# Replicating state-space channels: a stride of eight, in two transfers of 2 KB rows

## The chip, the cores and the metric

The kernel runs on one core of one Trainium2 chip. The metric is the device time of one execution in microseconds, the median over several runs. TensorE, VectorE, ScalarE and GpSimd (PE, DVE, ACT and POOL in the profile) compute; SyncE (SP) only issues DMAs, which run on the core's 16 DMA engines.

## The reference

The input `x` is [8, 256, 128]. It is normalised, and goes through two branches whose results are combined as `x + s * silu(f)`. One, `f`, is a six-layer local-attention transformer. The other, `s`, is one Mamba block, and it is the one that the change touches (D = 256 channels, N = 16 states, DTR = 16):

```
proj = h @ in_W + in_b
x1, g = (proj[..., :D], proj[..., D:])
...
dbc = x1 @ dbc_W + dbc_b
delta, Bm, Cm = (dbc[..., :DTR], dbc[..., DTR:DTR + N], dbc[..., DTR + N:])
delta = jax.nn.softplus(delta @ dup_W + dup_b)
A_disc = jnp.exp(delta[..., None] * A)
B_x = delta[..., None] * Bm[:, :, None, :] * x1[..., None]
...
def step(hc, inp):
    a, b = inp
    hc = a * hc + b
    return (hc, hc)
...
y = jnp.einsum('tbdn,btn->btd', hs, Cm)
y = jax.nn.silu(g) * y
out = y @ out_W + out_b
```

## The kernel before

Every engine has its own program, and semaphores order them. `start_phase` loads and normalises, `main_phase` does nearly all the work, `gate_phase` combines the branches. `main_phase` is a software pipeline over `i` in `FIRST_TO_LAST`: step `s` is one batch element in one of six layers, 48 steps in all, and each engine's loop body is a list, written out by hand, of calls such as `scores(i, 2)` or `z_decay(i - 7, 10)`. The attention of a step is, on TensorE, `qk` (L559), `value` (L575), four transposes `turn` (L584), `scores` (L596 and L604, 8 and 32 small matmuls in one call), `turn_p` (L616), `values_out` (L633, 32 small matmuls) and `w_out` (L648). Those many small matmuls make most of TensorE's 30944 instructions.

The Mamba branch is spread between them: batch `b` begins at step 6b. `du` holds, for each of the 128 partitions (channels c * 128 + p), 1024 numbers: the step sizes `delta` for two blocks c and 256 tokens, and then their products `u = delta * x1`. The scan has a row for each channel and state, so 16 channels at a time are replicated eight times over the partitions: `replicate(s, n)` on SyncE (L488 to L502) sends 16 rows of `du`, 4 KB each, to the 128 partitions of `rep[:, slot]`, partition 8d + z from row d, one DMA of 512 KB. There are eight of them for a batch, 64 in all, in four slots. `ROWS16` gives the order of the groups, and `chunk(j)` names, for each of 16 chunks, the group and which half of the 16 states the eight copies stand for. A slot is used by `z_decay` (ACT, L1015, exp of delta times A) and by `z_bu` (POOL, L1380, u times B); the semaphore `rep_in[slot]` goes up by 16 when a DMA has landed. Then come `z_scan` (DVE, L1215), `z_hc` (POOL, L1391) and `z_sum` (TensorE, L744), which sums the eight copies of a channel into a row of `Y`; `z_gate`, `z_out` and `z_state` finish the batch.

SyncE's list also holds `spread` (L422, 14 copies V<-V for a step, 64 KB each, before `values_out` can run), `arrange_x` (L436, XV<-XT), the weights of the next layer (L135 to L150) and `replicate_bc` (L482, L486), which doubles the rows of B and C from 8 to 128 partitions by a chain of DMAs; the last of them (64 partitions, `n = 4`) is issued just behind `replicate(·, 2)`, and POOL's first `z_bu` of a batch waits for it (semaphore `bc_in`). SyncE issues in order, and all its DMAs go through one queue of the profile, q1. TensorE's own instructions are also brought in by DMA: the profile lists them as q8, those of the other engines as q14.

Of the kernel before, what the change touches and what calls it, by code (L numbers as in the profile page):

```python
# [19 lines left out]
P = 128  # L20
LN_EXP = "natural_log_exp_and_others"
NB, SEQ, DM = 8, 256, 128
# [7 lines left out]
DI, NST, KC, DTR = 256, 16, 4, 16  # L30
DBLK = DI // P
# [8 lines left out]
BSTEP = 6  # L40
NAB = 12
NREP = 4
NH = 5
ZSUM = 2
ROWS16 = (0, 2, 4, 6, 1, 3, 5, 7)
# [243 lines left out]
def main_phase(nc, t, k, R, T, C0, X, M, Y):  # L289

    with ExitStack() as ctx:
# [42 lines left out]
        du = m.sb("du", [P, 2, DBLK, SEQ])  # L334
        delta, u = du[:, 0], du[:, 1]
        rep = m.sb("rep", [P, NREP, 2, DBLK, SEQ])
# [19 lines left out]
        rep_in = [m.sem(f"rep_in{n}") for n in range(NREP)]  # L356
# [15 lines left out]
        def is_batch(s):  # L372
            return 0 <= s < STEPS and s % BSTEP == 0

        def chunk(j):

            n = 2 * (j // 4) + j % 2
            return n, ROWS16[n], (j // 2) % 2
# [10 lines left out]
        def m_free(eng, kind, n, s):  # L389

            before = M_BEFORE[kind, n, s]
            if before is not None:
                kind, n, s = before
                b = s // BSTEP
                sem, count = {"z_x": (conv_done, b + 1), "z_g": (g_copied, 2 * b + 2), "z_dbc": (dbc_copied, b + 1),
                              "z_dup": (dx_copied, 2 * b + 2), "z_out": (st_done, b + 1),
                              "z_decay": (scan_done, 16 * b + n + 1)}[kind]
                eng.wait_ge(sem, count)
# [6 lines left out]
        block = ctx.enter_context(nc.Block())  # L405

        @block.sync
        def _(sp):
# [79 lines left out]
            def replicate(s, n):  # L488

                if not is_batch(s):  # L490
                    return
                b = s // BSTEP
                sp.wait_ge(delta_done, b + 1)
                k = 8 * b + n - NREP
                if k >= 0:
                    chunks = 16 * (k // 8) + 4 * (k % 8 // 2) + 3 + k % 2
                    sp.wait_ge(dA_done, chunks)
                    sp.wait_ge(bu_done, chunks)
                r = 16 * ROWS16[n]
                sp.dma_start(rep[:, (8 * b + n) % NREP].rearrange("p z c t -> p (z c t)"),  # L500
                             du[r:r + 16].rearrange("d (o z) c t -> d o (z c t)", o=1).broadcast_to([16, 8, 2 * DBLK * SEQ]))\
                  .then_inc(rep_in[(8 * b + n) % NREP], 16)  # L502

            for i in FIRST_TO_LAST:
                replicate(i - 4, 2)
                next_qk(i, 1)
                replicate(i - 7, 5)
                replicate_bc(i - 3, 0)
                replicate(i - 6, 4)
                replicate_bc(i - 4, 4)  # L510
                replicate(i - 3, 0)
                next_v(i, 0)
                arrange_x(i + 2)
                replicate(i - 7, 6)
                replicate(i - 7, 7)
                replicate_bc(i - 3, 1)
                replicate_bc(i - 3, 2)
                spread(i, 0)
                next_qk(i, 2)
                replicate(i - 5, 3)  # L520
                replicate(i - 3, 1)
                spread(i, 1)
                next_qk(i, 3)
                next_v(i, 1)
                spread(i, 2)
                next_qk(i + 1, 0)
                replicate_bc(i - 3, 3)
                spread(i, 3)
                other_weights(i)
# [293 lines left out]
        def _(act):  # L823
# [157 lines left out]
            def z_copy_dx(s):  # L981
                if not is_batch(s):
                    return
                b = s // BSTEP
                act.wait_ge(zu_full, b + 1)
                if b > 0:
                    for n in range(NREP):
                        act.wait_ge(rep_in[n], 16 * ((8 * b - n + NREP - 1) // NREP))
                for c in range(DBLK):
                    act.activation(delta[:, c, :], M[:, c * SEQ:(c + 1) * SEQ], ACT.Identity, bias=dupb[:, c:c + 1])\  # L990
                       .then_inc(dx_copied, 1)
# [13 lines left out]
            def z_decay(s, j):  # L1005

                if not is_batch(s):
                    return
                n = 16 * (s // BSTEP) + j
                r, rows, half = chunk(j)  # L1010
                act.wait_ge(rep_in[(8 * (s // BSTEP) + r) % NREP], 16 * ((8 * (s // BSTEP) + r) // NREP + 1))
                m_free(act, "z_decay", j, s)
                for c in range(DBLK):
                    col = 16 * c + 2 * rows + half
                    ins = act.activation(M[:, c * SEQ:(c + 1) * SEQ], rep[:, (8 * (s // BSTEP) + r) % NREP, 0, c, :], ACT.Exp,  # L1015
                                         scale=Aneg[:, col:col + 1])
                ins.then_inc(dA_done, 1)
# [3 lines left out]
            for i in FIRST_TO_LAST:  # L1021
                copy_p(i - 1, 3)
                copy_v(i, 1)
                z_decay(i - 8, 13)
                z_tap(i + 1)
                z_decay(i - 4, 1)
                z_decay(i - 6, 6)
                copy_qk(i, 0)
                copy_v(i, 2)
# [12 lines left out]
                z_decay(i - 5, 3)  # L1042
                square(i + 1, 2)
                z_copy_dx(i - 1)
                z_decay(i - 7, 8)
                z_exp_x(i)
# [246 lines left out]
        def _(pool):  # L1293
            links = [0]

            def link(ins):

                links[0] += 1
                ins.then_inc(pool_link, 1)
                pool.wait_ge(pool_link, links[0])  # L1300
# [55 lines left out]
            def z_delta(s):  # L1356

                if not is_batch(s):
                    return
                b = s // BSTEP  # L1360
                pool.wait_ge(ln_done, 2 * b + 2)
                if b > 0:
                    for n in range(NREP):
                        pool.wait_ge(rep_in[n], 16 * ((8 * b - n + NREP - 1) // NREP))
                link(pool.tensor_tensor(delta, delta, se[:], ALU.add))
                pool.tensor_tensor(u, delta, x1s[:], ALU.mult).then_inc(delta_done, 1)

            def z_bu(s, j):

                if not is_batch(s):  # L1370
                    return
                b = s // BSTEP
                n = 16 * b + j
                r, _, half = chunk(j)
                pool.wait_ge(rep_in[(8 * b + r) % NREP], 16 * ((8 * b + r) // NREP + 1))
                if j == 0:
                    pool.wait_ge(bc_in, BC_IN * (b + 1))
                if n >= NH:
                    pool.wait_ge(zy_full, (n - NH) // ZSUM + 1)
                pool.tensor_tensor(hb[:, n % NH], rep[:, (8 * b + r) % NREP, 1],  # L1380
                                   BC[:, 0, half:half + 1, :].broadcast_to([P, DBLK, SEQ]), ALU.mult).then_inc(bu_done, 1)
# [22 lines left out]
            for i in FIRST_TO_LAST:  # L1404
                z_hc(i - 6, 4)
                normalise(i, 0)
                normalise(i, 1)
                z_bu(i - 7, 8)
                z_hc(i - 8, 12)
                rotate_sum(i, 6)  # L1410
                z_bu(i - 4, 2)
                normalise(i, 2)
                z_bu(i - 7, 9)
                normalise(i, 3)
                normalise(i, 4)
# [34 lines left out]
                z_hc(i - 8, 15)  # L1450
                z_bu(i - 4, 3)
                z_delta(i - 2)
                z_bu(i - 4, 4)
                z_hc(i - 7, 11)
# [130 lines left out]
def mamba_vectors(g):  # L1585

    def cols(a):
        return a.reshape(-1, P, *a.shape[1:]).swapaxes(0, 1).reshape(P, -1)
    return np.concatenate([cols(g[n]) for n in ("in_b", "conv_b", "dup_b", "out_b", "rms_w", "conv_w")], 1)


def decay_rows(a):

    return a.reshape(DBLK, 8, 16, 2, 8).transpose(2, 4, 0, 1, 3).reshape(P, DBLK * NST)


def layer_vectors(g):

    v = np.zeros((P, DEPTH, NVEC), np.float32)
    for k, name in enumerate(("ln_g", "ln_b", "b2")):  # L1600
        v[:, :, k] = g[name].T
    for c, (f0, n) in enumerate(FFC):
        for h in range(2):
            v[:n, :, 3 + 3 * h + c] = g["b1"][:, h * FFI + f0:h * FFI + f0 + n].T
    return v
# [24 lines left out]
```

## Time and profile before

| | |
|---|---|
| median of 3 runs | 1931.85 us (1925.41 to 1934.93) |
| profiled execution, own time | 1930.3 us |
| its span | 1928.5 us |
| PE busy | 1756.7 us (91%) |
| DVE busy | 1596.1 us (83%) |
| POOL busy | 1527.8 us (79%) |
| ACT busy | 1252.5 us (65%) |
| TensorE's mean granted clock | 0.971 of full speed |
| DMA queue q1, share of 16 engines' span | 31.1% |
| rep<-du, 64 DMAs of 512 KB, issue to landing | 7.3 us |
| V<-V, 672 DMAs of 64 KB, issue to landing | 2.1 us |

Busy is the time in which an engine executes something; the shares are means over the whole span. A granted clock of 1.0 is 2.4 GHz and of 0.5 is 1.2 GHz. "issue" as the end of a wait means that the engine waited for nothing that the profile can name.

### The profile page before, as it was taken

What the parts mean: (1) busy time and instruction counts of PE and PEld (TensorE: products, weight loads), DVE (VectorE), ACT (ScalarE), POOL (GpSimd) and SP (SyncE); (2) the same over time, 40 slices, a digit from 0 to 9 for tenths busy, and PEclk for the clock granted to TensorE, in tenths of its full rate; (3) what the DMA queues carried; (4) which work ended last, traced back from release to release, by engine and by line L of the source; (5) the groups of instructions that cost most, each with busy time, mean ns of one, the idle gap of its engine ahead of it and who ended that gap; (6) DMA issues with size and microseconds to landing.
All of it is one profiled execution on the core that took longest, in us unless ns stands there. A gap on an engine that the chain in (4) does not pass through costs nothing. (4 is left out here: it accounts for less than half of the span.)

```text
span 1928.5 us, 73996 instructions
## 1 busy us (share of the span) xinstructions
PE 1756.7 (91%) x30944; PEld 999.4 (52%) x30944; DVE 1596.1 (83%) x2736; ACT 1252.5 (65%) x2339; POOL 1527.8 (79%) x1348
## 2 busy tenths in 40 slices
PE   3798999999999999999999999999999999999862
PEld 1355555555555555555555555555555555555420
DVE  5777998888888897889988898889878798888536
ACT  3566676676676676776776676676766666766630
POOL 1765899878998789878998789888888689987640
PEclk9999999999999999999999999999999999999975
DMA  3114234153313334142332433342331534123321
GB/s 109 29 39 70 45 71 79 37 85 49 66 33 67 72 61 71 41 71 55 68 71 37 87 49 59 74 79 39 67 58 33 100 62 63 30 45 58 54 23 44
DMA packets 95607, 113.14 MB, mean 59 GB/s; under 512 B 42334, under 2 KB 61548, under 8 KB 95276
## 3 DMA queue, kind: packets, MB, share of 16 engines
q1 hardware_dynamic: 95276, 108.41, 31.1%
q8 instruction: 246, 4.03, 0.9%
q14 instruction: 85, 0.70, 0.1%
HBM read 19.22 MB, written 1.05 MB: 11 GB/s over the span
## 5 line engine op out<-in xcount | busy, mean ns | idle before, releaser
L1315 POOL TENSOR_TENSOR AB<-qc,qn 128x512 f32<-128x512 f32 x384 | 494.6, 1298 | 21.4 <-DVE qn L1109 21.4
L1326 POOL TENSOR_TENSOR AB<-AB,rinv 128x512 f32<-128x512 f32 x384 | 402.0, 1062 | 24.5 <-DVE rinv L1132 24.5
L559 PE MATMUL bank<-wqkv,XT 128*128 128x512 f32 x768 | 400.2, 614 | 12.2 <-DVE qn L1109 12.2
L1333 POOL TENSOR_TENSOR Pb<-Pb,p_rden 128x512 f32<-128x512 f32 x192 | 200.1, 1042 | 235.2 <-DVE p_rden L1153 234.1
L848 ACT ACTIVATE qkT<-bank 128x512 f32<-128x512 f32 x384 | 229.2, 597 | 209.3 <-PE bank L584 208.6
L1109 DVE TENSOR_TENSOR qc<-bank,rt 128x512 f32<-128x512 f32 x384 | 261.3, 680 | 123.4 <-ACT sq L839 108.9
L584 PEld LDWEIGHTS bank<-ident,AB 128*128 128x128 f32 x1536 | 181.7, 142 | 181.9 <-issue 119.3
L839 ACT ACTIVATE sq<-bank 128x512 f32<-128x512 f32 x384 | 228.1, 594 | 66.4 <-PE bank L559 57.3
L1109 DVE TENSOR_TENSOR qn<-bank,rt 128x512 f32<-128x512 f32 x384 | 261.4, 681 | 0.0
L584 PE MATMUL bank<-ident,AB 128*128 128x128 f32 x1536 | 241.5, 280 | 13.3 <-ACT qkT L848 6.2
L1116 DVE TENSOR_REDUCE ssq<-sq 128x8 f32<-128x512 f32 x384 | 251.2, 670 | 0.0
L633 PEld LDWEIGHTS bank<-PT,V 64*64 64x64 f32 x12288 | 198.3, 135 | 76.1 <-issue 73.4
L633 PE MATMUL bank<-PT,V 64*64 64x32 f32 x12288 | 219.9, 221 | 13.5 <-issue 8.9
L575 PE MATMUL bank<-wqkv,XV 128*128 128x512 f32 x384 | 196.2, 613 | 3.0 <-DVE qn L1109 3.0
L863 ACT ACTIVATE PT<-bank 128x512 f32<-128x512 f32 x192 | 114.3, 595 | 121.9 <-PE bank L616 118.8
L604 PE MATMUL bank<-qkT 64*32 64x64 f32 x12288 | 167.2, 223 | 23.9 <-issue 23.9
L1215 DVE TENSOR_TENSOR_SCAN hb<-bank,hb 128x256 f32<-128x256 f32 x256 | 161.3, 672 | 29.2 <-ACT bank L1015 29.0
L648 PE MATMUL bank<-OT,wo 128*128 128x512 f32 x384 | 182.2, 598 | 2.4 <-DVE XT L1190 2.4
L1380 POOL TENSOR_TENSOR hb<-rep,BC 128x512 f32<-128x512 f32 x128 | 165.2, 1297 | 17.1 <-PE bank L744 8.6
L1391 POOL TENSOR_TENSOR hb<-hb,BC 128x512 f32<-128x512 f32 x128 | 162.2, 1275 | 20.3 <-DVE hb L1215 20.0
L1139 DVE TENSOR_REDUCE mx<-bank 128x8 f32<-128x512 f32 x192 | 130.3, 679 | 45.6 <-PE bank L604 43.0
L604 PEld LDWEIGHTS bank<-qkT 64*32 64x32 f32 x12288 | 151.3, 105 | 24.6 <-issue 24.4
(137 smaller groups left out, 2657.3 us busy)
## 6 DMA issues: line engine op xcount, KB each, us to landing
V<-V SPq DMA_DIRECT2D x672, 64.0 KB, 2.1
rep<-du SPq DMA_DIRECT2D x64, 512.0 KB, 7.3
wqkv<-in_Wqkv SPq DMA_DIRECT2D x36, 256.0 KB, 3.7
XV<-XT SPq DMA_DIRECT2D x96, 64.0 KB, 2.8
wo<-in_Wo SPq DMA_DIRECT2D x6, 512.0 KB, 4.1
BC<-BC SPq DMA_DIRECT2D x8, 256.0 KB
w<-in_W SPq DMA_DIRECT2D x6, 341.0 KB, 3.2
BC<-BC SPq DMA_DIRECT2D x8, 128.0 KB
```

The costliest lines, as they stand in the source:

```text
L559: pe.matmul(R[u % 2][:], XT[:, s % NB, (u % 2) * P:(u % 2 + 1) * P], wqkv[:, (u // 2) * 512:(u // 2 + 1) * 512], start=True, stop=True).th ...
L575: pe.matmul(R[n % 2][:], XV[:, q % 2, s % 2, tl, :], wqkv[:, c:c + 512], start=True, stop=True)\
L584: mm = pe.transpose(T[:, c * P:(c + 1) * P], AB[:, (8 * s + u) % NAB, c * P:(c + 1) * P], ident[:])
L604: mm = pe.matmul(SB[w * WIN:(w + 1) * WIN, odd, col:col + 2 * WIN], qkT[p0:p0 + DH, g % 2, c, WIN + tok:2 * WIN + tok], qkT[p0:p0 + DH, g ...
L633: mm = pe.matmul(OB[DH * odd:DH * (odd + 1), tl, c * P + w * WIN:c * P + (w + 1) * WIN], V[r, w, h0:h0 + DH], PT[r, g % 2, 2 * odd + c, w ...
L839: act.activation(sq[:, u % 2, :], R[u % 2][:], ACT.Square).then_inc(sq_done, 1)
L848: act.activation(qkT[:, g % 2, :, WIN + tl * P:WIN + (tl + 1) * P], T.rearrange("p (c t) -> p c t", c=4), ACT.Copy).then_inc(qkT_done, 1)
L1109: ins = dve.tensor_tensor(out if z == 0 else out[:, :, :, ::-1, :], src, tab, ALU.mult)
L1116: dve.reduce_sum(ssq[:, 8 * u:8 * u + 8], sq[:, u % 2, :].rearrange("p (h d) -> p h d", d=DH), AX_X)\
L1315: pool.tensor_tensor(AB[:, n % NAB, :], qc[:, u % 2, :], qn[:, u % 2, :], ALU.add).then_inc(rs_done, 1)
L1326: pool.tensor_tensor(o, o, r, ALU.mult).then_inc(nm_done, 1)
L1333: pool.tensor_tensor(Pb[:, g % 2], Pb[:, g % 2], r, ALU.mult).then_inc(pn_done, 1)
```

## The change

`replicate` takes the channels r, r + 8, ..., r + 120 of `du` instead of 16r to 16r + 15, and issues two DMAs instead of one: first `delta` (2 KB for each of the 128 rows), then `u` (2 KB). Both raise the same semaphore, so its waits count 32 for a slot instead of 16. What stands in which partition of `rep` has changed, so the host lays out the decay table, the gate's columns of `in_W` with their bias, and the rows of `out_W` in the new order; their sizes and loads stay as they are.

```
                 r = ROWS16[n]
                 for z in range(2):
                     sp.dma_start(rep[:, (8 * b + n) % NREP, z].rearrange("p c t -> p (c t)"),
                                  du[r::8, z].rearrange("d (o c) t -> d o (c t)", o=1).broadcast_to([16, 8, DBLK * SEQ]))\
                       .then_inc(rep_in[(8 * b + n) % NREP], 16)
...
-                        act.wait_ge(rep_in[n], 16 * ((8 * b - n + NREP - 1) // NREP))
+                        act.wait_ge(rep_in[n], 32 * ((8 * b - n + NREP - 1) // NREP))
...
-                pool.wait_ge(rep_in[(8 * b + r) % NREP], 16 * ((8 * b + r) // NREP + 1))
+                pool.wait_ge(rep_in[(8 * b + r) % NREP], 32 * ((8 * b + r) // NREP + 1))
...
-    return a.reshape(DBLK, 8, 16, 2, 8).transpose(2, 4, 0, 1, 3).reshape(P, DBLK * NST)
+    return a.reshape(DBLK, 16, 8, 2, 8).transpose(1, 4, 0, 2, 3).reshape(P, DBLK * NST)
+def sum_order():
+    return np.arange(P).reshape(16, 8).T.reshape(-1)
+def gate_order(a, axis):
+    block = [np.arange(DI + c * P, DI + (c + 1) * P)[sum_order()] for c in range(DBLK)]
+    return np.take(a, np.concatenate([np.arange(DI)] + block), axis)
...
+    laid["in_W"] = gate_order(given["in_W"], 1)
+    laid["out_W"] = given["out_W"].reshape(DBLK, P, DM)[:, sum_order()].reshape(DI, DM)
```

SyncE in the first batch, before: the DMAs as they stand in its program, each with its line, what it writes and reads, its shape, and how many in a row. Rep is the replicated slot, BC the rows of B and C, XV and V the attention's.

```order
 L482 DMA BC<-dbc 8x256 x4
-L500 DMA rep<-du 128x1x1024
-L486 DMA BC<-BC 8x1024
-L486 DMA BC<-BC 16x1024
-L422 DMA V<-V 32x512 x4
-L500 DMA rep<-du 128x1x1024
-L422 DMA V<-V 32x512 x7
-L486 DMA BC<-BC 32x1024
-L422 DMA V<-V 32x512 x3
```

The same place after the change:

```order
L501 DMA rep<-du 128x1x512 x2
L486 DMA BC<-BC 8x1024
L486 DMA BC<-BC 16x1024
L422 DMA V<-V 32x512 x4
L501 DMA rep<-du 128x1x512 x2
L422 DMA V<-V 32x512 x7
L486 DMA BC<-BC 32x1024
L422 DMA V<-V 32x512 x3
```

Nothing has changed its place; each rep<-du has become two, of half the row.

SyncE where the last three groups of the first batch are issued, between loads of weights, before:

```order
L500 DMA rep<-du 128x1x1024
L135 DMA wqkv<-in_Wqkv 128x512
L500 DMA rep<-du 128x1x1024 x2
L422 DMA V<-V 32x512 x4
L135 DMA wqkv<-in_Wqkv 128x2x256
```

and after:

```order
L501 DMA rep<-du 128x1x512 x2
L135 DMA wqkv<-in_Wqkv 128x512
L501 DMA rep<-du 128x1x512 x4
L422 DMA V<-V 32x512 x4
L135 DMA wqkv<-in_Wqkv 128x2x256
```

Here four DMAs stand back to back ahead of V<-V where two did. The orders of PE, ACT, DVE and POOL, and what each of their instructions waits for, are the same in both kernels.

## Rows read from the trace of the kernel before

**Rows 1.** Waits: engine line waited for: us in total, times, longest us.

```profile
PE bank L604 <- issue: 23.9, 14, 3.2
...
PE bank L633 <- issue: 8.9, 4, 3.6
...
PE bank L584 <- issue: 6.2, 3, 3.2
...
PE bank L633 <- DMA V<-V: 2.4, 2, 2.0
```

**Rows 2.** Timeline, PE: start us, us, engine line op, count [idle before <-releaser].

```profile
173.65 0.31 PE L604 MATMUL bank<-qkT 64*32 64x64 f32 x1 [3.25 <-issue]
...
186.50 0.72 PE L604 MATMUL bank<-qkT 64*32 64x64 f32 x36 [2.72 <-issue]
...
520.55 0.69 PE L604 MATMUL bank<-qkT 64*32 64x64 f32 x45 [2.87 <-issue]
...
1822.14 0.86 PE L633 MATMUL bank<-PT,V 64*64 64x32 f32 x23 [3.55 <-issue]
```

**Rows 3.** Timeline, SP, 164 to 178 us: issues (same columns).

```profile
164.67 0.59 SPq L500 DMA_DIRECT2D rep<-du  x1
165.31 8.57 SPq L422 DMA_DIRECT2D V<-V  x7
...
176.46 0.59 SPq L500 DMA_DIRECT2D rep<-du  x1
```

**Rows 4.** DMA view, 178.5 to 183 us: queue, kind, packets, MB, share.

```profile
q1 hardware_dynamic: 122, 0.46, 89.3%
```

**Rows 5.** DMA view, 183 to 185 us.

```profile
q1 hardware_dynamic: 804, 0.38, 80.4%
q8 instruction: 1, 0.02, 3.5%
q14 instruction: 1, 0.01, 1.5%
```

**Rows 6.** Windows: stretch, length, busy us (instructions) by engine, clock, DMA share, GB/s.

```profile
178.60:182.60 4.00, 4.00 (x77) 2.52 (x76) 2.55 (x5) 3.87 (x8) 2.74 (x4) 1.00 0.95 98
...
182.00:184.50 2.50, 1.78 (x39) 0.62 (x38) 1.79 (x3) 2.10 (x4) 1.36 (x2) 1.00 0.91 190
```

**Rows 7.** Windows behind the stops of rows 2.

```profile
173.20:176.70 3.50, 3.05 (x8) 1.79 (x9) 2.64 (x5) 0.69 (x2) 1.61 (x3) 0.51 0.55 129
...
1821.90:1828.70 6.80, 6.56 (x35) 2.66 (x34) 0.75 (x1) 1.09 (x2) 5.30 (x5) 0.50 0.01 2
```

**Rows 8.** Windows: one quiet step of each of the six places in a batch.

```profile
1170.00:1205.80 35.80, 35.60 (x646) 20.10 (x645) 30.83 (x51) 23.50 (x45) 33.83 (x31) 1.00 0.36 59
988.60:1027.60 39.00, 37.94 (x652) 20.86 (x651) 34.00 (x61) 29.75 (x57) 35.93 (x32) 1.00 0.18 42
1027.60:1063.00 35.40, 34.98 (x644) 19.90 (x642) 32.02 (x54) 24.61 (x48) 29.40 (x27) 1.00 0.23 34
845.10:880.20 35.10, 34.16 (x639) 20.42 (x640) 31.00 (x55) 25.32 (x46) 25.05 (x24) 1.00 0.53 90
880.20:915.10 34.90, 34.90 (x644) 20.50 (x642) 32.98 (x59) 22.84 (x44) 30.49 (x28) 1.00 0.20 52
1134.00:1170.00 36.00, 35.14 (x643) 20.39 (x643) 32.80 (x56) 28.67 (x54) 32.84 (x30) 1.00 0.32 57
```

**Rows 9.** Windows: the 20 long steps, first, last and their sum.

```profile
167.60:210.50 42.90, 36.53 (x635) 21.64 (x636) 30.78 (x52) 25.06 (x46) 25.02 (x23) 0.92 0.40 70
...
1732.00:1770.00 38.00, 34.36 (x639) 20.55 (x640) 30.97 (x53) 25.25 (x46) 24.98 (x23) 1.00 0.45 77
sum 769.70, PE 724.96 PEld 415.38 DVE 638.11 ACT 513.81 POOL 633.84; mean PE 36.25 PEld 20.77 DVE 31.91 ACT 25.69 POOL 31.69
```

**Rows 10.** DMA issues of the page: KB each, us from issue to landing.

```profile
V<-V SPq DMA_DIRECT2D x672, 64.0 KB, 2.1
rep<-du SPq DMA_DIRECT2D x64, 512.0 KB, 7.3
```

**Rows 11.** Waits, other engines and SP's own (same columns as rows 1).

```profile
POOL hb L1380 <- issue: 8.5, 7, 3.8
...
ACT du L990 <- DMA rep<-du: 5.2, 2, 2.9
...
SPq L422 <- ACT V L881: 635.5, 98, 23.6
```

More of the change, by code:

```diff
@@ L498, in replicate @@
                     sp.wait_ge(bu_done, chunks)
[L499 to L502, printed above, removed]
+                r = ROWS16[n]
+                for z in range(2):
+                    sp.dma_start(rep[:, (8 * b + n) % NREP, z].rearrange("p c t -> p (c t)"),
+                                 du[r::8, z].rearrange("d (o c) t -> d o (c t)", o=1).broadcast_to([16, 8, DBLK * SEQ]))\
+                      .then_inc(rep_in[(8 * b + n) % NREP], 16)
             for i in FIRST_TO_LAST:
@@ L1010, in z_decay @@
                 r, rows, half = chunk(j)
-                act.wait_ge(rep_in[(8 * (s // BSTEP) + r) % NREP], 16 * ((8 * (s // BSTEP) + r) // NREP + 1))
+                act.wait_ge(rep_in[(8 * (s // BSTEP) + r) % NREP], 32 * ((8 * (s // BSTEP) + r) // NREP + 1))
                 m_free(act, "z_decay", j, s)
@@ L1363, in z_delta @@
                     for n in range(NREP):
-                        pool.wait_ge(rep_in[n], 16 * ((8 * b - n + NREP - 1) // NREP))
+                        pool.wait_ge(rep_in[n], 32 * ((8 * b - n + NREP - 1) // NREP))
                 link(pool.tensor_tensor(delta, delta, se[:], ALU.add))
@@ L1619 @@
     laid["dbc_b"] = given["dbc_b"].reshape(-1, 1)
-    laid["mamba_vecs"], laid["layer_vecs"] = mamba_vectors(given), layer_vectors(given)
+    laid["mamba_vecs"], laid["layer_vecs"] = mamba_vectors({**given, "in_b": gate_order(given["in_b"], 0)}), layer_vectors(given)
     laid["A_rows"] = decay_rows(given["A_log"])
+    laid["in_W"] = gate_order(given["in_W"], 1)
+    laid["out_W"] = given["out_W"].reshape(DBLK, P, DM)[:, sum_order()].reshape(DI, DM)
     for short, a in {**laid, **constants()}.items():
```

## The prediction

> **What bounds the kernel now.** TensorE is busy for 91% of the span and is the nearest to a bound, so I read first what stops it. Most of its waits for another engine are short. What stands out are stops inside a single call, between small matmuls that depend on nothing in between: L604 14 times, 23.9 us; L633 four times, 8.9 us; L584 three times, 6.2 us; all "issue", up to 3.6 us long, and two more of L633 that end with a V<-V copy, 2.4 us [rows 1]. Together 41.4 us, nearly all in stops of 1.2 to 3.6 us, of which four are shown [rows 2].
>
> The times of these stops tell what they are. The one that ends at 173.65 us comes 9.0 us after a rep<-du was issued at 164.67, the one at 186.50 comes 10.0 us after that of 176.46 [rows 2, 3]. In the DMA view of 178.5 to 183 us, while that second transfer drains, there is q1 alone, at 89% of the 16 engines, and no q8 packet; in the next 2 us a q8 packet, TensorE's instructions, and a q14 one appear at once [rows 4, 5]. So I read the stop as TensorE running out of instructions: the block that it needs is asked for while the 512 KB transfer fills the DMA engines, and arrives when that has drained. The transfer drains slowly: 98 GB/s with the engines 95% busy [rows 6], so 524 KB / 98 = 5.3 us, of its 7.3 us from issue to landing [rows 10].
>
> A stop costs more than itself. After several of them TensorE's granted clock falls to the 1.2 GHz level: 0.51 in the 3.5 us behind the 3.25 us stop, 0.50 in the 6.8 us behind the 3.55 us one [rows 7]. The price in time I read from whole steps. A step, from the first L1142 of one `softmax(i, 0)` to the next, has a steady length when nothing is disturbed, which depends on its place in the batch of six: 35.8, 39.0, 35.4, 35.1, 34.9 and 36.0 us [rows 8]. Twenty steps are longer, 769.7 us in all [rows 9]. They fall on the six places 5, 2, 2, 5, 2 and 4 times, so undisturbed they would take 5 x 35.8 + 2 x 39.0 + 2 x 35.4 + 5 x 35.1 + 2 x 34.9 + 4 x 36.0 = 717.1 us. The excess is **52.6 us**. The stop at 1822.14 us lies in the tail, behind the last whole step: it costs 3.6 us and up to half of the 6.8 us at the lower clock [rows 2, 7], of which I count 5 in all. So 57.6 us, 3% of the kernel, hang on these stops.
>
> **Part by part.** *The stride.* How long a group's transfer drains when its 16 sources are eight partitions apart, no row shows. Bounds: not better than now, 98 GB/s; or as the last doubling of BC, whose sources are 64 partitions, with 190 GB/s in the window in which it drains [rows 6]. These rows differ in how widely the sources lie, which is just what the stride changes (the destinations are the same 128 partitions), so I take the second: 524 / 190 = 2.8 us, 2.5 us less for each of the 64.
>
> The Trainium skill (SBUF — State Buffer, Door 1: The DMA port swizzle) says that 16 neighbouring partitions reach 4 of the 16 ports, measured there at 104 GB/s, near this trace's 98; by its formula partitions r, r + 8, ..., r + 120 reach 8 ports, an estimate of 218 GB/s or 2.4 us. No run here shows it yet; the sum would move by under 3 us.
>
> *The split.* Two DMAs of 262 KB each have the same bytes. SP issues one more for each group, 0.59 us [rows 3], 64 x 0.59 = 38 us of SP's time, which lies beside 635 us in which SP only waits for V to be copied [rows 11]: nothing on the path, as long as the V<-V copies queued behind land in time (rival C). If the DMA engines take turns between queues only at a transfer's own end, an instruction block now waits for at most 1.4 us of rows instead of 5.3; I don't count on this and use the 2.5 us.
>
> *What a stop becomes.* A block that arrives 2.5 us earlier shortens a stop of g to max(0, g - 2.5). Of the stops, only five are longer than 2.5 us (3.25, 2.72, 2.87 and 3.55 [rows 2], and one of 3.2 at L584 [rows 1]): 0.75 + 0.22 + 0.37 + 1.05 + 0.7 = 3.1 us remain of 41.4, 7%. The clock behind the stops should stay at 2.4 GHz with them, since the lower level stood behind stops alone in the steps. I raise the part that stays from 7 to 15%, since all arrivals shift and blocks also meet the weights' and V's transfers: 0.85 x 57.6 = **49 us** gained.
>
> *The rest.* POOL's first `z_bu` of a batch waits for the last BC copy, which stands behind `replicate(·, 2)`: 8.5 us in seven waits; ACT waits 5.2 us for the last rep of the batch before [rows 11]. Both should all but go (each is under 2.5 us but one of 3.8 and one of 2.9). They lie beside TensorE's own work or within the long steps counted above, so I add nothing and keep them for the lower end. The consumers' order and all host-side reordering cost nothing: same loads, same shapes. Waiting for 32 instead of 16 costs nothing once both have landed, at about 4 us instead of 7.3 behind the issue. What is late next is DVE, at 31 to 34 us of work in a step of 35 to 39 [rows 8]: the steady steps are the floor of this gain.
>
> The sum: 1930.3 - 49 = 1881.3 us for the profiled execution; this lies 1.5 us under the median of the runs shown, so 1883 us.
>
> **Rivals.** *A: half.* The drain gets shorter, but stops with other causes take their place, or the steady steps don't come back because a step's place with weights loads stays slow. For it: the longest steps (42.9 us) had two stops and a change of clock in them, and alignment with the blocks is chance. Half of 57.6: 1903 us.
>
> *B: nothing.* The drain is set by the destinations or the DMA engines rather than the sources, or the stops have nothing to do with the transfer. Against it: 190 GB/s in rows 6, and the absence of q8 in rows 4. 1932 us, give or take 3. The Trainium skill (Runtime: NRT & Kernel Launch, Instruction fetch mechanics) says that fetching is in blocks of 16 KB and "mostly hidden"; by that rule alone TensorE would not stop for instructions and this rival would hold. The block's size agrees with the 0.02 MB of q8's one packet, the hiding does not agree with rows 2 and 5.
>
> *C: slower.* SP's additional issues hold back what stands behind them. In the long run of a batch's last three groups six DMAs now stand where three did, so V<-V is issued 3 x 0.59 = 1.8 us later, and if SP is held by the number of rows still in flight (it took 8.57 us for seven V<-V behind one rep, against 4.1 unhindered [rows 3]), by another 4.4 us for a group. That decides from the point where V<-V lands after `values_out` wants it, which happened twice before, 2.4 us [rows 1]. Price: 1.8 us in each of 8 batches is 14 us, on top of an unchanged drain: 1946 us; with the 4.4 us in part of the groups 1960. Against it: it needs the drain not to shorten, since what holds SP is what drains.
>
> **How the numbers follow.** The forecast (1867 to 1896) 0.68; A (around 1903) 0.14; B (1927 to 1937) 0.12; C (1940 to 1960) 0.06. The lower end: all 57.6 us and a third of the 13.7 us of the other waits gone, 1930.3 - 57.6 - 4.6 + 1.5 = 1869.6, and some microseconds below for steady steps that had hidden small delays, 1864. The upper end takes in A: 1912. A measurement of this kernel can tell about 0.5% from no change, 9.7 us: faster by more is the forecast and A, 0.82; within is B, 0.12; slower is C, 0.06.
>
> **What would show it.** In the profile after: rep<-du 128 DMAs of 256 KB, landing about 3 to 4 us behind their issue; a window over a draining pair at 170 to 220 GB/s instead of 98; L604, L633 and L584 with "issue" under 8 us together; mean granted clock from 0.971 to 0.98 or more; the steps at 35 to 39 us by their place with few longer; POOL's L1380 with hardly an idle gap; q1's share of the engines down from 31.1% to about 24%. Wrong would be: stops of 2 us and more inside L604 and L633 at 7 to 10 us behind a pair (then the cause is not the drain), or windows still at 98 GB/s (then the stride does nothing).

## The result, and the profile after

The changed kernel takes **1884.47 us** (median of 4 runs, 1882.02 to 1886.85), the kernel before 1931.18 us in the same comparison (1925.41 to 1934.93). The ratio is 0.9761, with a 95% interval from 0.9733 to 0.9788: 46.7 us less. The forecast was 1883 us. The profiled execution took 1884.55 us, its span is 1882.8 us.

The waits of TensorE come first, as in [rows 1]. L605, L634 and L585 after are L604, L633 and L584 before. This is the list of waits of the changed kernel (engine line waited for: us in total, times, longest us), the lines on these three with the rest left out:

```profile
PE bank L585 <- ACT qkT L849: 6.2, 9, 0.7
...
PE bank L634 <- DVE Pb L1143: 1.1, 2, 0.5
...
PE bank L634 <- issue: 0.2, 1, 0.2
```

L604's 14 stops with "issue", 23.9 us in all, have left the list; of L633's 8.9 us and its 2.4 us behind V<-V, 0.2 us remain; L584's 6.2 us with "issue" are gone (its 6.2 us behind ACT, short waits for another engine, stood in the list before as well). POOL's 8.5 us at L1380 with "issue" and ACT's 5.2 us for rep<-du [rows 11] are gone too.

One wait has grown: TensorE's for `normalise_p` on POOL, which scales the attention's weights `Pb`. The line of the kernel before stands first:

```profile
PE bank L616 <- POOL Pb L1333: 22.6, 31, 3.9
```

```profile
PE bank L617 <- POOL Pb L1334: 35.0, 43, 4.2
```

It is 33.0 to 36.0 us in every kernel below whose stops with "issue" are down to under 5 us, but for the one with the fast transfer beside (31.8). That fits a TensorE which, with fewer stops, comes earlier to values that POOL has not finished; one such place is shown below.

The transfers, from the DMA view and the page of the changed kernel (queue, kind: packets, MB, share of 16 engines; then issues: KB each, us to landing), against 31.1% before, and [rows 10]:

```profile
q1 hardware_dynamic: 104492, 108.41, 24.3%
q8 instruction: 246, 4.03, 0.9%
...
V<-V SPq DMA_DIRECT2D x672, 64.0 KB, 2.0
rep<-du SPq DMA_DIRECT2D x128, 256.0 KB, 4.0
```

The same bytes keep the DMA engines busy for about a quarter less time: 31.1% of 1928.5 us was 600 us, 24.3% of 1882.8 us is 458 us. The 4.0 us are the median over all 128 DMAs, first and second of a pair alike. Two windows in which a pair drains (stretch, length, busy us of PE, PEld, DVE, ACT and POOL with instructions, granted clock, DMA share, GB/s), against 98 GB/s [rows 6]:

```profile
166.30:168.30 2.00, 2.00 (x55) 0.91 (x56) 0.66 (x2) 1.54 (x4) 2.00 (x4) 1.00 0.94 192
175.70:177.70 2.00, 2.00 (x20) 0.99 (x22) 2.00 (x4) 1.97 (x3) 2.00 (x3) 1.00 0.99 192
```

The steps, in windows of the changed kernel, cut at the same instruction as in [rows 9]: the first, second, twelfth and last of the same twenty, and their sum.

```profile
169.60:204.50 34.90, 33.28 (x635) 19.63 (x636) 30.56 (x52) 25.28 (x46) 24.87 (x23) 1.00 0.31 70
311.30:353.50 42.20, 38.91 (x652) 21.64 (x650) 34.12 (x61) 30.07 (x57) 39.21 (x36) 0.96 0.26 66
...
1182.40:1225.80 43.40, 40.10 (x652) 22.21 (x649) 34.08 (x60) 29.99 (x57) 39.10 (x36) 0.92 0.25 63
...
1694.10:1729.10 35.00, 34.29 (x640) 20.51 (x641) 30.99 (x53) 25.23 (x46) 24.93 (x23) 1.00 0.29 68
sum 725.00, PE 709.01 PEld 409.23 DVE 638.65 ACT 513.42 POOL 627.59; mean PE 35.45 PEld 20.46 DVE 31.93 ACT 25.67 POOL 31.38
```

769.7 us have become 725.0, which is 44.7 of the 45.7 us between the two profiled spans. Of the rest, the tail behind the last whole step gave 4.8 us (158.5 to 153.7), and 3.8 us were lost elsewhere: the start, before the first of these steps, took 169.6 us instead of 167.6, and the other steps together 1.8 us more, all of it in one of them (below). Eighteen of them now have the length of the quiet steps [rows 8]; the first went from 42.9 to 34.9. Two did not come down to the quiet length, both at the second place in the batch, and they are looked at below.

### The profile page after: what moved, and what is told of

The parts are those of the page before. It is cut to its first block and busy times, and to the rows that moved or that the text cites. A ratio compares the mean times of both kernels' runs of the same rounds, so it can differ in the third digit from the quotient of the medians.

```text
span 1882.8 us, 74060 instructions
## 1 busy us (share of the span) xinstructions
PE 1744.8 (93%) x30944; PEld 995.9 (53%) x30944; DVE 1596.2 (85%) x2736; ACT 1253.1 (67%) x2339; POOL 1526.4 (81%) x1348
## 3 DMA queue, kind: packets, MB, share of 16 engines
q1 hardware_dynamic: 104492, 108.41, 24.3%
q8 instruction: 246, 4.03, 0.9%
## 5 line engine op out<-in xcount | busy, mean ns | idle before, releaser
L1327 POOL TENSOR_TENSOR AB<-AB,rinv 128x512 f32<-128x512 f32 x384 | 404.0, 1067 | 24.3 <-DVE rinv L1133 24.3
L585 PEld LDWEIGHTS bank<-ident,AB 128*128 128x128 f32 x1536 | 180.2, 141 | 174.5 <-issue 112.6
L585 PE MATMUL bank<-ident,AB 128*128 128x128 f32 x1536 | 239.0, 278 | 7.2 <-ACT qkT L849 6.2
L634 PEld LDWEIGHTS bank<-PT,V 64*64 64x64 f32 x12288 | 197.3, 135 | 64.3 <-issue 61.6
L634 PE MATMUL bank<-PT,V 64*64 64x32 f32 x12288 | 218.5, 220 | 2.2 <-DVE Pb L1143 1.1
L1381 POOL TENSOR_TENSOR hb<-rep,BC 128x512 f32<-128x512 f32 x128 | 165.5, 1298 | 9.6 <-PE bank L745 9.5
L605 PE MATMUL bank<-qkT 64*32 64x64 f32 x12288 | 164.0, 222 | 0.0
L560 PEld LDWEIGHTS bank<-wqkv,XT 128*128 128x128 f32 x768 | 122.9, 193 | 66.7 <-issue 30.2
L617 PE MATMUL bank<-ident,Pb 128*128 128x128 f32 x768 | 125.1, 286 | 35.0 <-POOL Pb L1334 35.0
```

The lines of the kernel that those rows point to most:

```text
L560: pe.matmul(R[u % 2][:], XT[:, s % NB, (u % 2) * P:(u % 2 + 1) * P], wqkv[:, (u // 2) * 512:(u // 2 + 1) * 512], start=True, stop=True).th ...
L585: mm = pe.transpose(T[:, c * P:(c + 1) * P], AB[:, (8 * s + u) % NAB, c * P:(c + 1) * P], ident[:])
L634: mm = pe.matmul(OB[DH * odd:DH * (odd + 1), tl, c * P + w * WIN:c * P + (w + 1) * WIN], V[r, w, h0:h0 + DH], PT[r, g % 2, 2 * odd + c, w ...
L1327: pool.tensor_tensor(o, o, r, ALU.mult).then_inc(nm_done, 1)
```

## The experiments

Eight kernels were run, each timed in the same way against the kernel before, which had medians of 1926.21 to 1929.03 us beside them. So the ratios compare better than the times.

**The stride alone.** One DMA, rows of 4 KB, from every eighth partition.

```
-                r = 16 * ROWS16[n]
+                r = ROWS16[n]
                 sp.dma_start(rep[:, (8 * b + n) % NREP].rearrange("p z c t -> p (z c t)"),
-                             du[r:r + 16].rearrange(...)
+                             du[r::8].rearrange(...)
```

> The stride alone: sources r, r + 8, ..., as in the change, but one DMA of 512 KB with 4 KB rows, as before. Theory 1 (only the length of the drain counts, and the sources' spread sets it): a window over a draining transfer shows about 190 GB/s instead of 98, landing about 4.5 us instead of 7.3, the stops inside L604 and L633 go, time 1881 to 1890 us. Theory 2 (the split does it: DMA engines turn to another queue when a transfer's share is done, so halving the transfer halves the wait, whatever the sources): the drain stays near 98 GB/s and the time near 1931 us. If both help, the drain is short but the longest waits are twice those of the change: a few stops of 1 us remain, 1886 to 1895 us.

1883.86 us (1876.62 to 1887.47), ratio 0.9759 [0.9719, 0.9800]. In its DMA view, and in two windows over draining transfers:

```profile
rep<-du SPq DMA_DIRECT2D x64, 512.0 KB, 4.8
```

```profile
168.20:170.20 2.00, 2.00 (x9) 0.98 (x7) 0.00 (x0) 1.80 (x4) 2.00 (x3) 1.00 0.98 191
178.00:180.00 2.00, 2.00 (x9) 0.87 (x7) 2.00 (x5) 1.98 (x3) 2.00 (x3) 1.00 0.99 188
```

Landing 4.8 us instead of 7.3, and of the stops one of 0.4 us is left, at L633. So the stride alone gives all that the change gives, and the split adds nothing that could be measured. Theory 1 held.

**The split alone.** Sixteen neighbouring sources, two DMAs.

```
                 r = 16 * ROWS16[n]
+                for z in range(2):
+                    sp.dma_start(rep[:, (8 * b + n) % NREP, z].rearrange("p c t -> p (c t)"),
+                                 du[r:r + 16, z].rearrange(...)
```

> The split alone: 16 neighbouring sources as before, two DMAs of 256 KB with 2 KB rows. Theory 1: the pair drains at 98 GB/s as before, 5.3 us for both, the stops stay, 1925 to 1937 us. Theory 2: an instruction block waits for one DMA's share at most, 2.7 us instead of 5.3, stops in L604 and L633 fall from 41 to under 10 us in all, and the time goes to 1884 to 1895 us although the drain is as long as before.

1906.42 us (1898.54 to 1913.22), ratio 0.9877 [0.9823, 0.9930]: half of the gain, outside the ranges of both theories. Its windows over two draining pairs, and its waits:

```profile
169.50:173.50 4.00, 3.34 (x80) 1.79 (x80) 3.96 (x8) 2.60 (x5) 2.21 (x3) 1.00 0.93 101
181.70:185.50 3.80, 3.80 (x100) 2.54 (x100) 3.54 (x6) 3.19 (x5) 1.98 (x2) 1.00 0.93 100
```

```profile
PE bank L605 <- issue: 12.6, 10, 2.1
POOL hb L1381 <- issue: 12.4, 7, 4.1
...
PE bank L585 <- issue: 4.8, 4, 2.1
PE bank L634 <- DMA V<-V: 3.3, 4, 2.0
PE bank L634 <- issue: 2.4, 2, 2.0
```

The drain is as slow as before, yet the stops are 23.1 us instead of 41.4, and the longest 2.1 us instead of 3.6. Something in the split shortens the wait without shortening the transfer, but by less than theory 2 said, which had under 10 us.

**The split, further.** Neighbouring sources, four DMAs with rows of 1 KB, `for z, c in ((0, 0), (0, 1), (1, 0), (1, 1))`.

> The split alone, further: 16 neighbouring sources as before, four DMAs of 128 KB with rows of 1 KB. With two DMAs (e2_split) the stops fell to half and the time to 1906 us, with the drain as slow as before. If an instruction block waits only for the DMA whose turn it is, 1.3 us of rows now instead of 2.7, the rest of the stops goes too: under 5 us in L605, L634 and L585, 1884 to 1894 us, with the windows still at about 98 GB/s and the waits for V<-V and BC as before. If the gain of e2_split had another cause, such as the earlier landing of delta, four parts add nothing and the time stays at 1898 to 1913 us.

1890.46 us (1884.66 to 1893.51), ratio 0.9804 [0.9769, 0.9840]. A window over a drain, and the waits:

```profile
170.80:174.80 4.00, 2.98 (x81) 1.79 (x80) 3.97 (x7) 2.90 (x5) 2.61 (x3) 1.00 0.86 100
```

```profile
POOL hb L1381 <- issue: 16.7, 7, 3.9
...
ACT du L991 <- DMA rep<-du: 5.5, 2, 3.1
...
PE bank L634 <- DMA V<-V: 3.7, 4, 1.2
...
PE bank L634 <- issue: 0.9, 2, 0.7
```

The drain is still at 100 GB/s, and what waits for data of a transfer waits as long as before or longer: ACT for rep 5.5 us, TensorE for V 3.7, and POOL 16.7 at L1381, where the first `z_bu` of a batch waits for the last BC copy. But the stops with "issue" in L605 and L585 are gone. So TensorE's stops were not late data. They get shorter with the length of one DMA's part of the drain: about 5.3 us with one DMA (41.4 us of stops), 2.7 with two (23.1), 1.3 with four (4.6, of which 3.7 are for V). That fits a block of instructions that waits until the DMA whose turn it is has passed. The profile doesn't show the moment at which a block is asked for, so the turn itself remains an inference.

There is a rival to it: each split also halved the rows, from 4 KB to 2 and 1 KB, and no run cuts a group in several DMAs with rows of 4 KB. The slow transfer below speaks for the DMA rather than the row: it is one DMA of 512 KB with rows of 2 KB, and stops of up to 3.4 us stand behind it, against 2.1 with two DMAs of the same row size and 3.6 before. Since it also follows a pair, this does not settle it.

This kernel lies 6 us above the change. TensorE's waits in these three places are 4.4 us longer (4.6 against 0.2); the intervals of the two ratios overlap.

**Sixteen of 32 neighbours.** As the change, from `du[r:r + 31:2, z]`, with r = 32 * (ROWS16[n] // 2) + ROWS16[n] % 2 and the host's tables laid out for it.

> As the change, two DMAs, but sources r, r + 2, ..., r + 30: 16 rows out of 32 neighbouring partitions. If the drain goes by how many of the ports of the SBUF the sources reach (the Trainium skill, SBUF - State Buffer, Door 1: The DMA port swizzle, says 8 for 32 neighbours as for a stride of eight), it is as short as with the stride of eight, about 190 GB/s, and the time 1881 to 1888 us. If it goes by how far apart the sources lie, the drain lies between, 100 to 150 GB/s, some stops stay, and the time is 1895 to 1930 us.

1884.03 us (1878.44 to 1886.62), ratio 0.9761 [0.9723, 0.9799]. Its DMA view:

```profile
q1 hardware_dynamic: 104492, 108.41, 24.2%
...
rep<-du SPq DMA_DIRECT2D x128, 256.0 KB, 4.0
```

and a window over its first draining pair:

```profile
165.00:167.00 2.00, 2.00 (x76) 1.00 (x74) 0.87 (x2) 1.50 (x3) 2.00 (x3) 1.00 0.92 192
```

A stride of two does the same as a stride of eight: same rate, same share of the engines, same landing, same time. So how widely the sources lie apart is not what counts, as long as they are not direct neighbours. This agrees with the Trainium skill (SBUF — State Buffer, Door 1: The DMA port swizzle), by which 32 neighbouring partitions reach the same number of ports, 8, as the stride of eight, and 16 neighbours only 4; the measured 192 and 98 GB/s stand to each other nearly as 8 to 4.

**A slow transfer that nobody reads.** The changed kernel with one DMA more for each group, from neighbouring partitions of a constant table to HBM.

```
+                sp.dma_start(aside[q % NREP],
+                             rot[0:16].rearrange(...).broadcast_to([16, 16, 512]))\
+                  .then_inc(aside_in[q % NREP], 16)
```

> The changed kernel, and behind each pair a DMA of 512 KB that nobody reads: 16 neighbouring partitions of the constant table rot, 16 times 2 KB each, to HBM. No engine's instruction waits for it (SP alone does, four groups later). If TensorE's stops are instruction blocks held up behind a slowly draining transfer, they come back though nothing that is computed has changed: 20 to 45 us of stops in L605, L634 and L585, time 1905 to 1940 us, and a window over it at about 98 GB/s. If the stops of the kernel before came from late data for the scan (rep) rather than from the drain, they stay away: 1880 to 1890 us, but for V and BC that land later, which would show as waits for a DMA.

1981.70 us (1980.17 to 1986.35), ratio 1.0284 [1.0250, 1.0317], 97 us over the change: more than any theory expected. A window over the draining transfer:

```profile
175.00:177.00 2.00, 2.00 (x8) 0.87 (x7) 2.00 (x5) 1.98 (x3) 2.00 (x3) 1.00 0.87 99
```

Its waits (L613 is `scores`, L642 `values_out`, L568 `qk`):

```profile
PEld bank L642 <- issue: 98.8, 191, 5.6
...
PE bank L642 <- DMA V<-V: 35.2, 8, 5.4
...
POOL hb L1389 <- issue: 24.2, 7, 4.3
...
PE bank L613 <- issue: 20.0, 10, 3.4
...
PEld bank L568 <- DMA wqkv<-in_Wqkv: 11.2, 4, 5.3
```

The stops inside L613 are back, 20.0 us in ten. But in this kernel data are late as well: TensorE waits 35.2 us for V<-V, and for weights. So only a part of the 97 us speaks for instruction blocks; the rest is data that queue behind the transfer.

The two kinds can be told apart in the trace, by whether a q8 packet, TensorE's instructions, begins in the 3 us before TensorE goes on. That q8 is TensorE's shows in the sizes: it carries 4.03 of the 4.73 MB of instructions, 85%, and TensorE has 84% of the instructions of all engines. Two places follow; the middle line is the DMA view of the 3 us that end with the first, and the 3 us ahead of the second hold no q8.

```profile
1579.05 0.42 PE L613 MATMUL bank<-qkT 64*32 64x64 f32 x3 [3.40 <-issue]
```

```profile
q8 instruction: 1, 0.02, 2.2%
```

```profile
646.08 1.19 PE L642 MATMUL bank<-PT,V 64*64 64x32 f32 x36 [5.37 <-DMA V<-V]
```

All ten stops of L613 and both "issue" stops of L642 have one such packet, none of the eight waits for V<-V has. In the kernel before, all 21 "issue" stops of [rows 1] have one, and so have the two that are put down to V<-V; in all these 23 places it begins 2.2 to 2.8 us before TensorE goes on. Of 368 other places of L604 and L633 in that kernel 32% have one in their 3 us. So these stops end with the arrival of instructions.

**The same bytes, fast.** `rot[0:128:8]` instead of `rot[0:16]`, nothing else.

> The same bytes to HBM and the same one more DMA in a group, but read from rows 0, 8, ..., 120 of rot. If the length of the drain decides and not the bytes or the number of DMAs, this one costs little: 5 to 15 us of stops, time 1884 to 1900 us. If the bytes decide, it costs the same as with neighbouring rows.

1887.96 us (1887.49 to 1888.85), ratio 0.9793 [0.9758, 0.9829].

```profile
aside<-rot SPq DMA_DIRECT2D x64, 512.0 KB, 6.0
...
PE bank L642 <- DMA V<-V: 2.5, 4, 1.3
PE bank L613 <- issue: 2.2, 3, 1.0
```

Against the changed kernel 33.6 MB more cost 3.5 us, which the intervals don't tell from nothing, when 16 spread partitions are read, and 97 us when 16 neighbours are. The two kernels differ in one subscript. Neither the bytes nor the number of DMAs is the cost, but how long they hold the DMA engines.

**Four DMAs with the stride.** The changed kernel with rows of 1 KB.

> The changed kernel with four DMAs for a group instead of two, rows of 1 KB: 128 more issues on SP, 2 x 0.59 = 1.2 us more in each group, the same bytes. If SP's issues are hidden, as predicted, 1881 to 1889 us. If they hold back V (the prediction's rival C), 1890 to 1910 us, with waits of L634 for V<-V. The drain may get longer if 1 KB rows are slower than 2 KB ones: then under 170 GB/s.

1881.71 us (1876.00 to 1886.38), ratio 0.9760 [0.9723, 0.9796]. SP's issues now take longer for each group, as its timeline shows (start us, us, engine line op, count), and still TensorE has no wait for V in its list:

```profile
163.18 2.51 SPq L501 DMA_DIRECT2D rep<-du  x4
165.73 5.30 SPq L422 DMA_DIRECT2D V<-V  x7
```

128 more issues than in the change cost nothing that can be measured. The prediction's rival C, SP holding back the copies, does not act at this size.

**Nearly no transfer.** The kernel before, but from the fifth group on only 64 of a row's 1024 numbers are replicated; the scan then computes with old numbers, every instruction stays.

```
+                    sp.dma_start(rep[:, (8 * b + n) % NREP, 0, 0, 0:64],
+                                 du[r:r + 16, 0, 0, 0:64].rearrange(...).broadcast_to([16, 8, 64]))
```

> The kernel before, but after the first four groups only 64 of the 1024 numbers of a row are replicated (32 KB instead of 512 KB), the rest of the slot stays as it is, so the scan computes with old numbers; every instruction of every engine stays. It shows what the transfers cost in all. Theory 1: the stops behind the transfers go, as with the change, and little more is to be had: 1877 to 1886 us. If the change still pays for its transfers (through late V copies, or through POOL's wait for BC), this is lower, 1860 to 1875 us. If the stops have nothing to do with the transfers: 1925 us or more.

1887.58 us (1887.23 to 1890.48), ratio 0.9786 [0.9751, 0.9821]. Taking nearly all of the transfers away is no faster than the change. The time is just above theory 1's range. What is left of stops:

```profile
PE bank L609 <- issue: 4.4, 2, 3.3
PE bank L638 <- issue: 0.4, 1, 0.4
```

(L609 and L638 are `scores` and `values_out`.) The two of L609 stand behind groups that are sent in full, in the first of the twenty long steps, which keeps most of its excess, 40.1 us where the change has 34.9 (same columns as above):

```profile
169.20:209.30 40.10, 35.23 (x636) 20.83 (x637) 30.79 (x53) 25.41 (x46) 25.11 (x23) 0.96 0.43 77
```

Without these 5.2 us this kernel would stand at an estimated 1882.4 us, within the range of the change (1882.02 to 1886.85). So the change already gets nearly all that was to be had from these transfers.

## Why the prediction was right

*The stops as the thing to read.* Right. They were 41.4 us in places with no dependency, 39.0 of them "issue", and the steps that held them were 52.6 us too long [rows 1, 8, 9]; 44.7 us of that came back with the stops. The tail, counted at 5 us, gave 4.8.

*The stops as instruction blocks behind the drain.* Supported from four sides: they vanish with a shorter drain (the stride), they vanish with a drain as long but cut in four, while the waits for data stay, some come back behind a transfer that nobody reads, and each of them ends 2 to 3 us after the begin of a q8 packet, while the waits for V behind the slow transfer do not. The distances were read too narrowly: 9 and 10 us from issue to the end of the stop were two cases; where two or three rep<-du stand in a row, the stop ends up to 14 us behind the last of them.

*The drain.* 2.8 us at 190 GB/s came true, with windows of 192, and a median landing of 4.0 us, at the end of the 3 to 4 us that were foreseen. The way to it was partly luck. The row of BC's last doubling, [rows 6], also differs in that it reads 64 partitions and writes 64, and its window holds other traffic: 508 of its 592 packets are under 512 B, from the XV<-XT copies. And the reason given, how widely the sources lie, is not the one that acts, as the stride of two shows.

*The split* was priced at nothing on the path, and that held for the change. But the sentence beside it, that a block may wait for one DMA's part only, was not counted on, and it is where the working was too cautious: alone the split takes 1.2% off the time (ratio 0.9877), the change 2.4%. The rule for what a stop becomes does not carry over to it: a block 2.7 us earlier would leave some 3 us of the stops, and 23.1 us stayed. Since the stride and the split take away the same stops, their gains don't add.

*What stays.* The sum kept 15%, 8.6 us, for new stops. About that much of the excess did stay, 725.0 - 717.1 = 7.9 us, but not as the prediction put it: no new stop stands behind a transfer. It is in two steps at the second place of a batch, 42.2 and 43.4 us instead of 39, which were 42.3 and 41.5 us before. The step that failed is the comparison with [rows 8] there, which put their whole excess down to the stops. Three places of TensorE's timeline show it: the first of the two steps before, the second before, and the second after the change.

```profile
325.83 0.63 PE L616 MATMUL bank<-ident,Pb 128*128 128x128 f32 x4 [2.01 <-POOL Pb L1333]
```

```profile
1211.28 1.15 PE L604 MATMUL bank<-qkT 64*32 64x64 f32 x60 [1.58 <-issue]
```

```profile
1190.91 1.08 PE L617 MATMUL bank<-ident,Pb 128*128 128x128 f32 x4 [2.10 <-POOL Pb L1334]
```

In the first step the wait for POOL was there before the change and is there after it (2.10 us). In the second a stop of 1.58 us has gone and the wait for POOL has come in its place, and the step is 1.9 us longer. A third step at this place, which was quiet before and is none of the twenty, went the same way: it holds a wait of 1.76 us for POOL and a mean clock of 0.96 after the change, and takes 40.8 us instead of 39.0. Around this wait the clock is at the 1.2 GHz level and POOL is busy without a gap (windows of the changed kernel, same columns as above):

```profile
319.50:322.90 3.40, 3.07 (x7) 1.93 (x8) 3.39 (x7) 2.79 (x5) 3.40 (x4) 0.51 0.42 99
...
1189.90:1196.70 6.80, 5.79 (x32) 3.32 (x36) 6.58 (x12) 4.35 (x7) 6.80 (x7) 0.50 0.38 90
```

So these steps lose their time to POOL and to the clock. That the total came out within 2 us of the forecast owes something to this: a remainder of the right size for another reason.

*The clock.* Half right. In the other eighteen steps it now stays at 2.4 GHz. But "the lower level stood behind stops alone in the steps" was a misreading: in the kernel before it also fell behind the 2.01 us wait for POOL above, to a mean of 0.61 in the 4 us from 326 us on. The mean granted clock went only from 0.971 to 0.973, not to the 0.98 that was named. The three steps are one reason. The other is the start, nearly all of which lies ahead of the first group's transfer (windows of the kernel before and of the changed one):

```profile
0.00:167.60 167.60, 117.70 (x2024) 68.48 (x2024) 117.66 (x229) 85.79 (x164) 94.60 (x97) 0.97 0.25 58
```

```profile
0.00:169.60 169.60, 121.59 (x2024) 70.35 (x2024) 117.64 (x229) 85.78 (x164) 94.63 (x97) 0.94 0.24 60
```

The same instructions, 3.9 us more of TensorE's time at a lower clock. This differs between kernels that are alike there: the stride of two had 0.98 in its first 167 us, a mean clock of 0.979, and 1878.44 us in that execution. Why it differs is open.

*The rivals.* A (half) was the split's result, not the change's, but a part of its mechanism acts: other waits take the stops' place, the 12.4 us more for `normalise_p`. They made two steps longer than before, those above, by 1.9 and 1.8 us. B (nothing) fell with the first window at 192 GB/s. C (slower through SP) was tested with twice the issues and did not act; what it describes, late V<-V, is real once transfers drain slowly enough, as the slow transfer beside showed with 35.2 us.

## What to carry to other kernels

In this kernel a DMA from 16 SBUF partitions that sit next to each other held the DMA engines nearly twice as long for its bytes as one from 16 partitions that are every second or every eighth, and the loss appeared far from it: not only at whoever reads the data, but as stops with no cause inside an engine that runs through many instructions. Look for waits called "issue" between independent instructions, see whether they end behind the drain of a large transfer (here 8 to 14 us after the last one's issue) and shortly after a packet of that engine's instruction queue, and if so spread the transfer's source rows over more partitions, or cut it in parts if the layout can't be changed.

Price a step by comparing it with quiet steps at the same place of the loop, but check that what disturbs it is the same thing in each: two of twenty here were long for another reason as well.

## What the runs showed of the hardware that was not expected

Cutting a transfer in parts shortens how long TensorE waits for instructions though the drain is as long: at 98 to 101 GB/s, one, two and four DMAs for a group, with rows of 4, 2 and 1 KB, gave 41.4, 23.1 and 4.6 us of stops. Sources two partitions apart and eight apart drain alike, 24.2 and 24.3% of the engines' time and 4.0 us to landing. And reading 16 neighbouring partitions instead of 16 spread ones, in a transfer that no one needs, moved the whole kernel by 94 us, from 1887.96 to 1981.70 us.
